# One attention-and-convolution network on one core: behind the last attention, who makes the float32 normalized values, and in what order ScalarE and GpSimd work

## What is computed

```python
x = x + attention(gn(x))      # f, g, h projections; softmax(f^T g) over i; gamma * (h beta)
x = x + pairs_conv(gn(x))
# pairs_conv:
y = relu(bn(w1 @ x + b1))             # 256 -> 32 channels, per pixel
packed = y[rows] * y[cols]            # all 528 products of two of the 32 channels
z = relu(bn(w2 @ packed + b2))        # 528 -> 256 channels
```

## Time and profile before

| | us |
|---|---|
| median of 3 runs | 2282.79 (2282.22 to 2282.92) |
| the profiled execution's own time | 2280.18 |
| its span, first to last instruction | 2278.4 |
| busy in the span: PE / PEld | 2210.3 (97%) / 1628.1 (71%) |
| busy: DVE / ACT / POOL | 1876.7 (82%) / 1668.2 (73%) / 630.2 (28%) |
| mean granted PE clock | 0.995 of full speed |
| the last attention step's matmuls end at about | 2173 |

### The profile page before, as it was taken

One profiled execution on the slowest core, in us unless ns is written; L12 is line 12 of the kernel. 1 busy time (PEld: TensorE's weight loads), 2 busy tenths in 40 slices (PEclk: granted clock), 3 DMA queues, 4 the chain that ended last, 5 costly groups with the idle time before them and its releaser, 6 DMA issues.

```text
span 2278.4 us, 42578 instructions
## 1 busy us (share of the span) xinstructions
PE 2210.3 (97%) x16782; PEld 1628.1 (71%) x16782; DVE 1876.7 (82%) x3113; ACT 1668.2 (73%) x2692; POOL 630.2 (28%) x607
## 2 busy tenths in 40 slices
PE   4899999999999999999999999999999999999978
PEld 3677777777777777777777777777777777777733
DVE  7788888888888888888888888887888877787688
ACT  5577777777777777778777777777777777777856
POOL 2100111112222333234522133333432222222244
PEclk9999999999999999999999999999999999999989
DMA  5000000000012222220122221222101111111101
GB/s 195 11 1 1 1 8 8 8 17 1 20 43 66 66 68 55 66 57 26 56 61 67 62 58 49 55 68 59 39 20 39 36 34 34 29 34 34 34 24 65
DMA packets 57096, 95.48 MB, mean 42 GB/s; under 512 B 8416, under 2 KB 15264, under 8 KB 56864
## 3 DMA queue, kind: packets, MB, share of 16 engines
q1 hardware_dynamic: 56896, 92.76, 14.5%
HBM read 67.03 MB, written 19.14 MB: 38 GB/s over the span
## 4 chain that ended last, share of the span: by engine, by line
PE 91%; DVE 6%; ACT 1%; issue 1%; SPq 0%; DMA 0%; POOL 0%; DVEq 0%; ACTq 0%
PE acc L1496 19%; PE acc L1503 19%; PE acc L1497 19%; PE tps L1334 10%; PE sps L1350 9%; PE tps L1386 3%; PE acc L1328 3%; PE tps L1388 2%; PE tps L1372 1%; DVE mx L686 1%; PE tps L1365 1%; PE acc L1386 1%; DVE xn L667 1%; DVE pl L705 1%; PE tps L1315 1%
## 5 line engine op out<-in xcount | busy, mean ns | idle before, releaser
L1121 ACT ACTIVATE ph<-sps,esc 128x512 f16<-128x512 f32 x1024 | 703.0, 686 | 408.0 <-PE sps L1350 403.3
L1496 PE MATMUL acc<-hth,ph 128*128 128x257 f16 x4096 | 955.8, 274 | 6.6 <-ACT ot L1127 6.6
L1497 PE MATMUL acc<-htl,ph 128*128 128x256 f16 x4096 | 955.0, 273 | 0.0
L686 DVE TENSOR_REDUCE mx<-tps 128x1 f32<-128x512 f32 x1024 | 701.2, 687 | 298.0 <-PE tps L1334 292.8
L705 DVE TENSOR_TENSOR pl<-p,ph 128x512 f16<-128x512 f32 x1024 | 807.5, 789 | 35.1 <-ACT p L1122 34.1
L1122 ACT ACTIVATE p<-sps,esc 128x512 f32<-128x512 f32 x1024 | 698.4, 682 | 0.0
L1503 PE MATMUL acc<-hth,pl 128*128 128x257 f16 x4096 | 620.0, 273 | 0.0
L1503 PEld LDWEIGHTS acc<-hth,pl 128*128 128x128 f16 x4096 | 399.8, 98 | 159.3 <-issue 0.3
L1497 PEld LDWEIGHTS acc<-htl,ph 128*128 128x128 f16 x4096 | 401.0, 98 | 150.2 <-issue 0.3
L948 POOL TENSOR_TENSOR xl<-xn,xh 128x512 f16<-128x512 f32 x176 | 229.1, 1323 | 862.3 <-DVE xn L667 836.5
L1496 PEld LDWEIGHTS acc<-hth,ph 128*128 128x128 f16 x4096 | 401.1, 98 | 76.5 <-issue 9.5
(11 more groups left out here) (216 smaller groups left out, 1575.5 us busy)
## 6 DMA issues: line engine op xcount, KB each, us to landing
rt<-turned SPq DMA_DIRECT2D x96, 256.0 KB, 4.2
xt<-x SPq DMA_DIRECT2D x36, 512.0 KB, 3.7
xb<-x SPq DMA_DIRECT2D x32, 512.0 KB, 4.2
out<-zt SPq DMA_DIRECT2D x47, 256.0 KB, 2.1
rt<-turned SPq DMA_DIRECT2D x72, 64.0 KB, 4.7
turned<-yb SPq DMA_DIRECT2D x24, 96.0 KB, 1.9
out<-fst SPq DMA_DIRECT2D x8, 256.0 KB, 2.0
out<-htl SPq DMA_DIRECT2D x8, 256.0 KB, 2.0
```

Source lines behind the costliest of these rows:

```text
L686: V.reduce_max(mx[:, tile, c:c + 1], tps[par][:], AX).then_inc(t_free[par], 1)
L1121: A(ph[:, u % SLOTS], sps[u % 2][:], ACT.Exp, scale=esc[:]).then_inc(ph_ok, 1)
L1496: mm(acc[j][:, 0:C + 1], w, hth[:, t], start=(t == 0), stop=False)
L1497: mm(acc[j][:, 0:C], w, htl[:, t], start=False, stop=False)
```

## The change

ACT makes the float32 values of chunks 2 to 7 of the last image's second layer, in two halves put at two places of its order. DVE keeps those of chunks 0 and 1. On ACT a turn is now: `product_high` 0 of chunk n + 1, `high` of c + 3, `product_high` 1, `normed` half 0, `z_out` half 0 of chunk n - 1, `product_high` 2, `y_out` and `halves_high` of n + 2, `normed` half 1, `z_out` half 1 of chunk n - 1, `product_high` 3 and 4. On POOL `low` of chunk 2 goes ahead of the two residuals of chunk 23. On PE `project_y` of chunks 24 and 25 both come before the first two `turned_channels`. On DVE, besides the loss of six `normed`, `product_low` 3 of chunk 23 goes behind the bias.

```diff
--- before.py
+++ after.py
@@ -232,7 +232,7 @@
         JOBS.extend(("second", LASTB, c) for c in range(NCH))
         JOB = {job: i for i, job in enumerate(JOBS)}
 
-        BY_ACT = [("first", 0, c) for c in range(2, NCH)]
+        BY_ACT = [("first", 0, c) for c in range(2, NCH)] + [("second", LASTB, c) for c in range(2, NCH)]
         BY_DVE = {job: sum(j not in BY_ACT for j in JOBS[:i + 1]) for i, job in enumerate(JOBS)}
 
         THROUGH = []
@@ -885,18 +885,18 @@
             moments(1, LASTB)
             product_low(SHARED - 1, 0)
             variance(1, 0)
-            for grp in range(1, 4):
+            for grp in range(1, 3):
                 product_low(SHARED - 1, grp)
             bias(second_norm(LASTB), 1)
             dve.wait_ge(gn_ok, second_norm(LASTB) + 1)
             normed(("second", LASTB, 0))
-            product_low(SHARED - 1, 4)
+            for grp in range(3, 5):
+                product_low(SHARED - 1, grp)
             normed(("second", LASTB, 1))
             halves_low(SHARED)
             product(SHARED, 0)
             product(SHARED, 1)
             product_low(SHARED, 0)
-            normed(("second", LASTB, 2))
             for grp in range(2, 5):
                 product(SHARED, grp)
                 product_low(SHARED, grp - 1)
@@ -905,8 +905,6 @@
             for c in range(NCH - 1):
                 n = SHARED + c
                 product(n + 1, 0)
-                if c + 3 < NCH:
-                    normed(("second", LASTB, c + 3))
                 for grp in range(1, 5):
                     product(n + 1, grp)
                     product_low(n + 1, grp - 1)
@@ -1033,9 +1031,9 @@
             power(second_norm(LASTB), 1)
             for c in range(2):
                 low(("second", LASTB, c))
+            low(("second", LASTB, 2))
             for h in range(H2):
                 residual(SHARED - 1, h)
-            low(("second", LASTB, 2))
             for c in range(NCH):
                 if c + 3 < NCH:
                     low(("second", LASTB, c + 3))
@@ -1092,12 +1090,20 @@
                     last = A(xh[:, k % RING, h], src, ACT.Identity, bias=nbias[layer][:, h:h + 1],
                              scale=rstd[layer][:, h:h + 1])
                 last.then_inc(xh_ok, 1)
-                if job in BY_ACT:
+                if kind == "first" and job in BY_ACT:
+                    for h in range(H2):
+                        normed(job, h)
+
+            def normed(job, h):
+
+                kind, b, c = job
+                layer, k = int(kind == "second"), JOB[job]
+                if h == 0:
                     act.wait_ge(xl_ok, k - 1)
-                    for h in range(H2):
-                        last = A(xn[:, k % 2, h], xb[0][:, h, c * CH:(c + 1) * CH], ACT.Identity,
-                                 bias=nbias[0][:, h:h + 1], scale=rstd[0][:, h:h + 1])
-                    last.then_inc(xa_ok, 1)
+                ins = A(xn[:, k % 2, h], xb[b % 2][:, h, c * CH:(c + 1) * CH], ACT.Identity,
+                        bias=nbias[layer][:, h:h + 1], scale=rstd[layer][:, h:h + 1])
+                if h + 1 == H2:
+                    ins.then_inc(xa_ok, 1)
 
             def qk_high(b, c, bank):
                 par = qk_set(b, c)
@@ -1235,28 +1241,38 @@
                 z_out(SHARED - 1, h, acc[2 + h])
             y_out(SHARED, tps[0])
             halves_high(SHARED)
-            product_high(SHARED, 0)
             high(("second", LASTB, 2))
-            product_high(SHARED, 1)
+            for grp in range(2):
+                product_high(SHARED, grp)
+                normed(("second", LASTB, 2), grp)
             y_out(SHARED + 1, tps[0])
             halves_high(SHARED + 1)
             for grp in range(2, 5):
                 product_high(SHARED, grp)
-            for c in range(NCH):
+            for c in range(NCH - 1):
                 n = SHARED + c
-                if c + 3 < NCH:
+                more = c + 3 < NCH
+                product_high(n + 1, 0)
+                if more:
                     high(("second", LASTB, c + 3))
-                if c + 1 < NCH:
-                    product_high(n + 1, 0)
-                    product_high(n + 1, 1)
+                product_high(n + 1, 1)
+                if more:
+                    normed(("second", LASTB, c + 3), 0)
+                if c:
+                    z_out(n - 1, 0, acc[2 * ((c - 1) % 2)])
+                product_high(n + 1, 2)
                 if c + 2 < NCH:
                     y_out(n + 2, tps[0])
                     halves_high(n + 2)
-                if c + 1 < NCH:
-                    for grp in range(2, 5):
-                        product_high(n + 1, grp)
+                if more:
+                    normed(("second", LASTB, c + 3), 1)
+                if c:
+                    z_out(n - 1, 1, acc[2 * ((c - 1) % 2) + 1])
+                for grp in range(3, 5):
+                    product_high(n + 1, grp)
+            for n in range(B * NCH - 2, B * NCH):
                 for h in range(H2):
-                    z_out(n, h, acc[2 * (c % 2) + h])
+                    z_out(n, h, acc[2 * (n % 2) + h])
 
         @block.tensor
         def _(pe):
@@ -1580,9 +1596,8 @@
                 pe.wait_ge(xl_ok, JOB["second", LASTB, c] + 1)
                 for i in range(H2):
                     project_y(n, i, tps[0])
-                if c == 0:
-                    for grp in range(2):
-                        turned_channels(n, grp)
+            for grp in range(2):
+                turned_channels(SHARED, grp)
             for grp in range(2, 5):
                 turned_channels(SHARED, grp)
             turned_channels(SHARED + 1, 0)
```

## The result

| | before | changed |
|---|---|---|
| median of 9 runs on one chip, us | 2282.22 (2280.66 to 2282.92) | 2288.94 (2286.13 to 2290.59) |
| ratio, 95% interval | | 1.0029 (1.0020 to 1.0038) |
| profiled execution: own time / span, us | 2280.18 / 2278.40 | 2288.19 / 2286.4 |
| tail: first write of `xb` by DVE after the last attention, to the end | 103.41 | 109.58 |

The changed kernel is 6.7 us slower by the medians. Both kernels do the same up to the tail, and the start of the tail scatters by itself (2174.16 to 2177.45 us over all profiles of this study; 2174.99 and 2176.82 in these two), so I compare the tails of the two profiles: **+6.17 us**. I cut them at the starts of `product` 0 of the chunks.

A forecast was written before the change was run, and what follows sets the result against it. Before the change, DVE was taken to pace four tail chunks and PE the last two. Beginning 0.9, first loop 1.3, four periods 3.5 and end 0.3 gave +6.0 us on 2282.79: 2288.8 us, range 2280.0 to 2291.5.

The forecast's parts named there:

- The loop closes through ACT and DVE: Tail periods: ACT's list of 7.64 us plus 2.09 back over DVE gives 9.7 us without holds, above PE's 9.06.
- Two holds, one after the other: Tail periods: POOL's residual holds `product_low` 3, its `low` then `product_low` 4; period 11.3 us, +3.5 us over four.
- one hold only: Rival, tail periods: POOL doesn't get between `product_low` 3 and 4; period 10.4 us, total 2285.2; chance 0.20.
- ACT waits over 2 us, is busy 8.3; PE idles 2.2: Signs per tail period that would show the forecast right: ACT's group 0 waiting on DVE, ACT's busy time, PE's idle time.
- The beginning, +0.9: Tail opening: POOL's second residual of chunk 23 holds `halves_low` of chunk 25, ending at 2200.65 instead of 2199.76; +0.9 us.
- The first loop, +1.3: Up to `product` 0 of chunk 26: POOL holds two DVE operations; +1.3 us, between 1.0 and 1.7.
- two ends: First loop: `product` 0 of chunk 26 starts 6.9 us after `project_y` if DVE is first, 7.7 if POOL; before 5.95.
- The end, +0.3: Chunk 31: `turned_channels` waits for a `halves_low` held by chunk 28's second residual; 7.3 us instead of 7.0, +0.3 us.
- Faster by moving work off the busiest engine: Rival, tail periods: ACT's loop closes under 9.06 us and PE becomes the bound; -5.4 us, total 2277.4; chance 0.14.
- The clock: Rival, tail periods: PE's granted clock falls for a chunk, its matmuls take up to twice 9.06 us; 2294 or above; chance 0.04.

The follow-up runs named there:

- run 1: Changed kernel with POOL's `low` of chunks 3 to 7 and residuals of chunks 24 to 29 on 2 of 512 columns; 2280.01 us, ratio 0.9992.
- Runs 3: Changed kernel with ACT running `high` of chunk c + 3 ahead of `product_high` 0; 2284.71 us, ratio 1.0007.
- run 4: Changed kernel with ACT running `high` and both `normed` halves of chunk c + 3 ahead of `product_high` 0; 2280.69 us, ratio 0.9992.
- run 2: Changed kernel with POOL starting `low` of chunk c + 3 only after DVE's `product` 0 of the chunk after next; 2297.56 us, ratio 1.0067.
- run 8: Changed kernel with POOL's two residuals of chunk 23 back ahead of `low` of chunk 2; 2287.52 us, ratio 1.0024.
- run 6: Kernel before with the whole new opening (chunk 2 on ACT, new orders on ACT, DVE, POOL, PE) but the old loop; 2282.76 us, ratio 1.0003.
- run 5: Run 4 with ACT's and POOL's old opening, chunk 2 on DVE, and in POOL's loop `low` ahead of both residuals; 2282.64 us, ratio 1.0001.
- run 12: Run 5 with run 4's order on POOL in the loop and PE's old order; 2280.33 us, ratio 0.9991.
- run 7: Kernel before with only PE's order changed, `project_y` of chunks 24 and 25 before the first two `turned_channels`; 2282.09 us, ratio 0.9996.

## Why the prediction was right, point by point

The forecast was 2288.8, the median 2288.94, and the tail grew by 6.17 us for a forecast 6.0. That the two medians meet within 0.14 us is partly luck. The 6.0 were added to a median of three runs, 2282.79; nine runs of the same kernel gave 2282.22, and by these the change is 6.7. The terms are the better test, as the second table has them:

- *The loop closes through ACT and DVE.* Right. ACT's list from group 0 to group 4 was walked as 7.64 us, and the way back as 2.09: 9.7. Without POOL's holds it measured 9.86 (run 1). Runs 3 and 4 confirm it from the other side: the same work in another place of ACT's order makes 11.36 into 10.02 and 9.44.
- *Two holds, one after the other.* Right, and this was the weakest link, since the trace of before showed it for L667 only. `product_low` 3 took 1.34 (walked: 1.31), `product_low` 4 1.53 (1.64), together 2.90 us from the start of one to the end of the other (2.88). The rival "one hold only" would have had group 4 at 0.68. Period 11.36 against 11.3.
- *ACT waits over 2 us, is busy 8.3; PE idles 2.2.* 3.17, 8.16 and 11.36 - 9.26 = 2.10. The prediction didn't say where PE idles: it waits 0.96 us per period for `low`, and later 0.91 for `halves_low`. `low` ends where it was walked (6.48 us behind `halves_high`, walked 6.47), and nobody waits for the `project_y` behind it. The expectation of run 2 put `low` some 3 us later and took this slack as enough, which it wasn't.
- *The beginning, +0.9.* Measured +1.01, by the hold that was named (`halves_low` of chunk 25, 1.63 us) and, by run 8, from the order that was named.
- *The first loop, +1.3.* This term had two ends, and I took the middle. DVE was first, so the lower one held: `halves_low` 1.52 and `product_low` 3 0.93 are the held ones, `product_low` 2 at 0.69 is not. For that end the walk gives 6.9 - 5.95 = 0.95, measured 1.13, of which a little is the clock. With the clock back at the same place the holds are worth 1.04: run 8 has 12.78 against 11.74 before (both back at 28 us), and the second profile of the changed kernel 13.82 against 12.77 in run 6 and 12.78 in run 1 (all three at 32). In run 1 the two held operations take 0.71 and 0.68 instead of 1.53 and 0.93. By that second profile, set beside the kernel before, the term would be +2.1, outside the 1.0 to 1.7 that I had allowed: the later clock was worth as much as the holds, and the walk took the clock as fixed. So it is partly luck that the first profile came so close in this term.
- *The end, +0.3.* 0.28, by the hold that was named: `halves_low` of chunk 31 takes 1.73 us beside the second residual of chunk 28, and `turned_channels` 0 of chunk 31 starts 7.28 us behind `product` 0 of chunk 30 (walked 7.3).
- *Faster by moving work off the busiest engine* (the rival with 0.14). The rule stood beside it: the Trainium skill, Perfetto Trace Analysis, section Optimizing Scalar/DVE Operations, says that with DVE saturated it may make sense to move some work to ScalarE. The trace doesn't bear that out as a rule by busy time: DVE was relieved and the period grew from 10.42 to 11.36. With the same operations in ACT's hole (run 4) it fell to 9.44, so the advice holds only with the place.
- *The clock* (0.04). It stayed at 1.00 in the loop with waits of 0.96, 0.91 and 0.22 us per period. Run 2 shows that the rival was no idle one: there, behind a wait of 1.78 us, the clock fell.

Other misses stand beside this, all in expectations. The large ones are run 2 (the slack of `project_y`, the place of the first hold, and the clock), run 5 (the holds moved instead of going) and run 12, which kept run 4's periods but not the earlier beginning (tail 102.84, expected 100.5 to 102.5). Run 6 and the first profile of run 7 had tails 2.4 and 1.7 us longer than before, where up to 1.3 and 0.3 were expected, both with a late clock. Two small ones: run 1's tail fell by 6.35 us (6.5 to 8 expected), run 8's by 1.07 (0.6 to 0.9).

What stays open is what decides when the clock comes back. That the clock makes most of the spread between runs of one kernel is likely, since every run has its mean granted clock on record and the two go together: of the 33 runs of the kernel before beside runs 5 to 8, the ten at 0.995 took 2280.41 to 2281.30 us and the 22 at 0.993 took 2282.09 to 2285.22. Of the nine of the changed kernel the five at 0.994 or 0.995 took 2286.13 to 2289.20, the four at 0.992 or 0.993 took 2288.94 to 2290.59. Part of that lies far ahead of the tail, as the two profiles of the kernel before showed, and has nothing to do with the change.

## What to carry to other kernels

Look for the loop that closes from one engine's late operation through another back to the first one's early operation, and add up its latencies; an engine that is busy 7 of 10 us can still have no room at the place where work is put, and the room is where it waits for the other. When one engine's operations stop another's, moving them doesn't remove the stop: find which operation will be next to it, and prefer one that nobody waits for. And where an effect is 0.3% of the run, cut the trace by periods and repeat the profile before believing a single stretch.

## What the runs showed of the hardware that was not expected

**The clock comes back at different moments in executions of one kernel.** During the opening, in which PE waits several times (in the profile of before 2.91 and then 5.08 us for `halves_low`), the clock falls to 0.50, some 17 to 21 us behind the tail's start (in run 12 once more at 24), and it returns to 1.00 during the first loop. In windows of 1 us, counted from the tail's start, the first one at 1.00 is that from 28 us in both profiles of before, in run 8 and in the second profile of run 7; from 30 us in the first of the changed kernel; from 31 in run 12; and from 32 in the other eight. All four at 28 have the residuals of chunk 23 in their old place, as three of the later ones do; none of the seven with the new order is at 28. So the new opening may have a part in it, which no run here settles. But one program alone has both. Two stretches of the kernel with PE's order alone, the same program twice (columns as above; 27.0 to 29.0 and 29.0 to 31.0 us behind the tail's start; first the profile with 13.30, then that with 11.75):

```profile
2202.32:2204.32 2.00, 2.00 (x6) 0.41 (x5) 0.44 (x2) 0.00 (x0) 1.46 (x2) 0.50 0.01 4
2204.32:2206.32 2.00, 2.00 (x6) 0.58 (x4) 1.35 (x2) 0.63 (x1) 0.81 (x1) 0.50 0.00 0
```

```profile
2204.21:2206.21 2.00, 2.00 (x8) 0.60 (x7) 0.73 (x3) 0.00 (x0) 1.45 (x2) 0.79 0.01 4
2206.21:2208.21 2.00, 2.00 (x10) 0.74 (x9) 2.00 (x4) 0.63 (x1) 0.82 (x1) 1.00 0.00 0
```

PE was busy throughout in all four. The later return costs 13.30 - 11.75 = 1.55 us there (32 against 28 us), and in the changed kernel 13.82 - 12.87 = 0.95 (32 against 30).

**The clock fell inside a busy loop** (run 2) after a wait of 1.78 us, the second of its kind, one period behind a wait of 1.67 us that left it at 1.00; the waits of 0.96, 0.91 and 0.22 us per period in the changed kernel never moved it. It was back within 4 us, and fell again in each of the two periods that followed (mean 0.87), each with a wait of 1.79 us. No other run had a wait of that length in the loop; the longest is 1.29 us, before, at a clock of 1.00.

**DVE and POOL take turns between operations that follow each other at once.** `product_low` 3 and 4 stand 0.03 us apart on DVE, and POOL's `low` still comes between them (1.34, then 1.53). The Trainium skill, SBUF — State Buffer, section SBUF: two separate sides, has the one that starts first keep the shared ports for its whole instruction; the rows agree with that, and add who is next: the one that has been waiting. DVE's L752, which reads PSUM, takes 0.67 to 0.70 us beside POOL or not: that of 2227.57 above stands in POOL's `low` pair (2225.40 to 2228.56).
